# Gated linear attention on one core: the key-value product moved ahead of the query-key product in every turn

## The reference, cut to what matters

```
q, k, v = (x @ Wq.T), (x @ Wk.T), (x @ Wv.T)          # each as (b, s, 16, 64)
log_decay = -softplus(x @ Wd.T + bd)
k_gated = k * sigmoid(x @ Wg.T)
s_t = exp(log_decay_t) * s_{t-1} + k_gated_t^T v_t      # the state, one per head
o_t = q_t s_t
out = o * rsqrt(mean(o*o) + eps) * norm_w
out = out * sigmoid(x @ Wog.T)
return out @ Wo.T
```

## Time and profile before

| | |
|---|---|
| median of three runs | 2803.56 us |
| lowest and highest of them | 2798.45 and 2810.31 us |
| the profiled execution | 2810.31 us, span 2808.5 us |
| PE busy over the span | 86% |
| mean granted clock of PE, as a share of full speed | 0.922 |

### The profile page before, as it was taken

The page is one execution under the profiler, slowest core; times in us unless marked ns, Lnnn a source line. Parts: engine busy times, 40 slices in busy tenths (PEclk is TensorE's granted clock), DMA queues, the critical chain, the costliest instruction groups (busy, mean ns, idle before and its releaser), DMA issues. The chain is left out here.

```text
span 2808.5 us, 35462 instructions
## 1 busy us (share of the span) xinstructions
PE 2412.8 (86%) x14123; PEld 1671.5 (60%) x14131; DVE 1471.8 (52%) x2517; ACT 862.3 (31%) x1247; POOL 505.0 (18%) x420
## 2 busy tenths in 40 slices
PE   5877775778888979988999998839999799999888
PEld 3655663432222767865667666736667577777764
DVE  7996876558774340125564564571110355455543
ACT  1111556424556112324442432201221232222132
POOL 3332330040001113420100001102221210101010
PEclk8989887988999979999999999859999899999999
DMA  3001100054340016633321221032231300000000
GB/s 111 1 0 65 42 16 16 7 125 90 63 63 26 14 62 236 235 114 105 96 64 64 87 73 33 25 114 72 100 101 57 106 18 17 12 12 17 1 33 30
DMA packets 73254, 177.16 MB, mean 63 GB/s; under 512 B 16759, under 2 KB 36728, under 8 KB 67545
## 3 DMA queue, kind: packets, MB, share of 16 engines
q1 hardware_dynamic: 60562, 123.00, 15.4%
q0 software_dynamic: 10368, 50.01, 5.2%
q10 hardware_dynamic: 2176, 2.10, 0.2%
HBM read 149.45 MB, written 25.43 MB: 62 GB/s over the span
## 5 line engine op out<-in xcount | busy, mean ns | idle before, releaser
L1621 PE MATMUL L_ffn_h_ps<-L_ffn_xgT,L_ffn_w 128*128 128x512 f32 (+2 forms) x992 | 232.5, 391 | 6.7 <-DVE L_ffn_xgT L1704 5.7
L1633 PE MATMUL L_ffn_y_ps<-L_ffn_w,L_ffn_h 128*128 128x256 f32 x1008 | 222.5, 380 | 4.8 <-issue 3.9
L526 DVE TENSOR_REDUCE L_attn_neg<-L_attn_Y 128x1 f32<-128x512 f32 (+3 forms) x304 | 187.4, 658 | 59.0 <-PE L_attn_Y L399 57.5
L1633 PEld LDWEIGHTS L_ffn_y_ps<-L_ffn_w,L_ffn_h 128*128 128x128 f32 x1008 | 189.7, 190 | 33.1 <-issue 8.2
L1679 ACT ACTIVATE L_ffn_h<-L_ffn_h_ps,L_ffn_w 128x640 f32<-128x640 f32 (+2 forms) x184 | 101.5, 552 | 347.4 <-PE L_ffn_h_ps L1621 321.7
L1621 PEld LDWEIGHTS L_ffn_h_ps<-L_ffn_xgT,L_ffn_w 128*128 128x128 f32 x992 | 154.4, 193 | 84.2 <-issue 69.3
L496 ACT ACTIVATE L_attn_room<-L_attn_Y 128x1024 f32<-128x1024 f32 (+1 forms) x192 | 147.4, 812 | 82.3 <-PE L_attn_Y L450 81.6
L399 PE MATMUL L_attn_Y<-L_attn_K,L_attn_Q 104*128 104x512 bf16 (+3 forms) x384 | 120.6, 365 | 44.1 <-DVE L_attn_neg L526 24.9
L1713 DVE TENSOR_TENSOR L_ffn_yg<-L_ffn_y_ps,L_ffn_w 128x256 f32<-128x256 f32 x63 | 26.7, 425 | 223.5 <-PE L_ffn_y_ps L1633 223.5
L1704 DVE COPY L_ffn_xgT<-L_ffn_t_ps 128x256 f32<-128x256 f32 x63 | 24.6, 421 | 215.1 <-PE L_ffn_t_ps L1608 199.8
L1754 POOL DMA_INDIRECT token_outputs<-L_ffn_yg,puts x63 | 61.8, 981 | 325.3 <-DVE L_ffn_yg L1713 325.3
(11 more groups left out here) (561 smaller groups left out, 4977.1 us busy)
## 6 DMA issues: line engine op xcount, KB each, us to landing
L_ffn_w<-in_L_ffn_w SPq DMA_DIRECT2D x8, 2180.0 KB
L_attn_bc<-decays SPq DMA_DIRECT2D x32, 512.0 KB, 5.9
L_attn_bp<-decays SPq DMA_DIRECT2D x32, 256.0 KB, 6.8
L_attn_Q<-L_attn_q_parts SPq DMA_DIRECT2D x48, 128.0 KB, 4.7
L_attn_K<-L_attn_k_parts SPq DMA_DIRECT2D x48, 128.0 KB, 6.7
L_attn_first_w<-in_L_attn_w SPq DMA_DIRECT2D x8, 640.0 KB
L_attn_w<-in_L_attn_w SPq DMA_DIRECT2D x8, 640.0 KB, 3.9
token_outputs<-zero SPq DMA_DIRECT2D x1, 4096.0 KB, 20.6
```

The lines of the kernel that those rows point to most:

```text
L526: nc.vector.tensor_reduce(neg[:, c, j0:j0 + heads, tt], R[n % 2][:, 0:heads * width(tt, c)].rearrange("p (h k) -> p h k", h=heads), X_AXIS ...
L1621: ins = nc.tensor.matmul(h_ps[f % 2][:, lo // CW, 0:hi - lo], w1[g % NB][:, kt, f * P:(f + 1) * P], xgT[u][:, kt, lo:hi], start=kt == 0, s ...
L1633: ins = nc.tensor.matmul(y_ps[k % 2][:], h[:, f, t * P:(t + 1) * P], w2[g % NB][:, f, :], start=f == 0, stop=f == FT - 1)
```

## The change

In the table JOBS, `kv` moves from third place to first, and the buffers are dealt anew: `kv` goes to X2 where `s0` was, and `s0` to X3 where `kv` was. The waits that `buffer_read` derives follow: `kv` now waits for the read of `og` from X2, and the pair s0/s1 for the read of `kt` from X3. On DVE the masking of kv moves ahead of the two multiplications of s0 and s1, and the wait for `read["kt"]`, which is DVE's own, goes. No instruction is added, removed or resized.

```
-        JOBS = [("s0", 0, 2), ("s1", 0, 0), ("kv", 0, 3), ("q", 1, 1), ("g", 1, 2), ("k", 1, 3), ("out", 0, 0),
+        JOBS = [("kv", 0, 2), ("s0", 0, 3), ("s1", 0, 0), ("q", 1, 1), ("g", 1, 2), ("k", 1, 3), ("out", 0, 0),
                 ("v", 1, 1), ("og", 1, 2), ("kt", 1, 3)]
...
                 if has_this:
-                    dve.wait_ge(read["kt"], n + 1)
+                    dve.wait_ge(mm["kv"], n + 1)
+                    V.tensor_tensor(kv[:], chunks(X[BUF["kv"]])[:, 0:CH - 1, :], over(same[:], CH - 1), ALU.mult).then_inc(read["kv"], 1)
                     for j in range(2):
                         dve.wait_ge(mm["s1"], n + 1)
                         V.tensor_tensor(bc[par][j][:], chunks(X[BUF[f"s{j}"]]), bc[par][j][:], ALU.mult).then_inc(read[f"s{j}"], 1)
-                    dve.wait_ge(mm["kv"], n + 1)
-                    V.tensor_tensor(kv[:], chunks(X[BUF["kv"]])[:, 0:CH - 1, :], over(same[:], CH - 1), ALU.mult).then_inc(read["kv"], 1)
                     past(dve, mm["out"], n)
```

## The result

| | before | after |
|---|---|---|
| median of five runs, us | 2803.56 | 2819.90 |
| lowest and highest, us | 2798.45, 2810.31 | 2814.05, 2822.70 |
| ratio after / before, 95% interval | | 1.0053 (1.0032 to 1.0075) |
| the profiled execution, us | 2810.31 | 2812.25 |

The changed kernel is slower, by 16.3 us from median to median; the interval of the ratio makes that 9 to 21 us. The forecast was 2820. The profiled execution of the changed kernel is not one of the five. In a second comparison on another occasion it was 2817.84 against 2800.72, ratio 1.0060 (1.0046 to 1.0074). The two profiled executions differ by only 1.9 us, and that would mislead: the part with the change lengthened by 21 us while the rest of the program, which the change doesn't touch, was 19 us shorter in the one than in the other.

A forecast was written before the change was run, and what follows sets the result against it. PE was taken to bound each turn by its instructions plus its waits. Terms 13.9 + 0 + 2.0 + 0.5 = 16.4 us slower, on the median of 2803.56, gave 2820 us; range 2808 to 2834.

The forecast's parts named there:

- The wait of kv: Behind the transposes, kv waits for kd: 1.43 us idle in place of 0.44, in 14 turns, 13.9 us (13.2 to 16.1).
- The neighbours: Durations of s and kv on PE in their new order: taken as unchanged, up to 1.7 us either way over 14 turns.
- Turn 0: First turn, kd late: s no longer hidden in kv's gap, 2.0 us more (1.5 to 3.6).
- Turn 15: Last turn: out waits for states that DVE makes after reading s and kv, 0.5 us more (0.3 to 0.8).
- The sum: All terms over this part of the program: 16.4 us slower.
- the main term: Middle-turn borders where kv waits for kd: 14 x 0.99 = 13.9 us slower.
- Not exposed: PE begins s while kv waits, so s covers kd as now: 2803.6 us, no loss; chance 0.05.
- DVE late: Multiplications and states shift by 1.0 us, v waits 0.3 to 0.5 us in 15 turns: 2826 us; chance 0.12.
- The room left: Slack between DVE's scaled query and the start of v after the change: forecast as 0.2 us.
- The clock falls at each border: Each wait ahead of kv costs clock, 1.63 us in 14 turns: 39 us slower in all, 2843 us; chance 0.07.
- Given back elsewhere: Slow-clock pattern behind the part falls differently; if 8 us come back, the time is 2812 us; chance 0.16.

The follow-up runs named there:

- the one with an instruction more: Changed kernel with one extra DVE instruction, half the size of kd and its result unused, ahead of kd; one run took 2840.72 us.
- the deal alone: Kernel before with s0 dealt to X3 and kv to X2 as in the changed kernel, s still first; one run took 2819.92 us.
- the run with the late mask: Changed kernel with DVE masking kv behind the two multiplications and its own wait for the kt read as before; one run took 2830.30 us.
- before with two instructions more: Kernel before with two extra DVE instructions, each about 0.60 us and unused, ahead of kd; one run took 2802.24 us.

## Why the prediction was right, and where its terms were not

*The wait of kv* was predicted as 1.43 us in place of 0.44, 14 times. It is 1.43, 14 times, in both traces of the changed kernel, and the 0.10 us of way was right too. That the cover of s is the cause is shown: the same delay of `kd` costs nothing where s stands before kv and 0.60 us where kv is bare, and the cover ends where it was put, at about 1.0 us.

*The neighbours* were taken as zero, with 0.12 us either way. They cost 27.24 - 26.09 - 0.99 = 0.16 to 0.17 us a turn, 2.3 over 14, where the bound was 1.7. This is the term that was mis-sized, and the trace had rows for it only in the old order. Why kv takes 0.07 and the projections 0.10 more in the new order is open.

*Turn 0* was put at 2.0 (1.5 to 3.6). From the start of the transposes to `out` it takes 21.3 and 21.7 us in the traces of before, 24.4 and 24.6 after: 3.0. The gap grew to 6.9 and 7.5 us, and kv and s together take 6.0 and 5.8 us in place of 1.73 + 1.99 = 3.72, so the slow stretch costs 2.3 and 2.0 where it cost 1.6 before: in the direction of the upper end. The term itself varies from trace to trace; kv first in the old buffers, with a gap of 6.0, took 23.6.

*Turn 15* was put at 0.5 more, by a chain of 8.96 us from kv to `out`; it is 1734.19 - 1725.31 = 8.88, where before the start of s and that of `out` lay 8.41 apart: 0.47. The wait of `out` is 5.09 and not about 5.3, against 4.59 before, and `out` is slow behind it, as it was before. The timeline of PE after, which answers to the earlier trace rows:

```profile
1734.19 3.33 PE L2336 MATMUL L_attn_X<-L_attn_qd,L_attn_st 128*128 128x128 f32 x14 [5.09 <-DVE L_attn_st L2459]
1737.45 3.33 PE L2341 MATMUL L_attn_X<-L_attn_bc,L_attn_va 128*64 128x128 f32 x32
```

From there to the part's last transposes it is 48.4 and 48.2 us after, 46.7 and 44.1 before: 2.9 more. The longer wait is not the reason that the traces bear out: kv first in the old buffers has the same 5.09 and takes 45.5, and the one with an instruction more has it too and takes 44.4, while the deal alone, with 4.59, takes 45.8. How the slow stretches fall there differs from trace to trace.

*The sum.* 14 x 1.155 = 16.2, then 3.0 and 0.5 make 19.7, where the traces have 19.6 up to the last `out`; the forecast had 16.4 for the same terms, some 3 us too little, of which the neighbours are 2.3 and turn 0 is 1.0. The measured time is 16.3 and in the second comparison 17.1, and both intervals (9 to 21 and 13 to 21 us) hold 16.4 as well as 19.6. So that the median came out within 0.1 us of the forecast is luck; the direction, the place and the main term were right on their own.

*The rivals.* Not exposed: refuted, in every turn. DVE late: it did not happen, and the run with the late mask shows that 1.2 us more would have cost 0.7 to 0.8 a turn. The room left was 0.53 us, or 0.4 less the 0.1 for the way, where 0.2 had been forecast. The clock falls at each border: it did not, the granted clock is 1.00 from 1320 to 1722; but one step further, at 2.03 us, it falls behind 5 waits of 14. The prediction's own evidence was better than it said: the 0.97 of the earlier trace rows comes from its last 4 us (0.70 from 541 to 545, behind a wait of 2.17 us), while from 500 to 541, with the waits of 1.35 us, the clock is 1.00. The section of the Trainium skill weighed there ("TensorE: Matmul & The Clock Gate", "A second HAM failure mode: psum-queue depth-cycling") has the clock swing where small idle times stand between groups of matmuls. The traces agree with it at 2.03 us, and at 3.82, if that is still small; they do not at 1.43 to 1.58, where none of 70 waits in five traces was followed by a lower clock. Given back elsewhere: seen in the first pair of traces, and not separable from chance.

## What to carry to other kernels

On an engine that takes its work in order, the job placed right behind the maker of another engine's input should be one that needs neither that engine's result nor the buffer it is reading; here such a job of 1.99 us covered a way there and back of 1.43. When buffers are dealt by a table, read off for each job which reader it waits for: a wait that comes from the buffer and not from the data can be dealt away. And when a prediction is met, compare the part and not only the whole.

## What had not been expected of the hardware

The start of s at a border comes 0.25 us behind the engine that ends its wait, be it ACT or DVE: it began 0.26 us after ACT's gate and, with the deal alone, 0.25 after DVE's `kd`, where kv needs 0.10 behind the same `kd`. The prediction had laid the 0.26 on ACT. What makes the difference is open; in turn 8 s and kv alike start 0.05 us after the last x_tok listed.

Without any wait the period fell by 0.51 us and not by 0.44. From the start of the transposes to that of s it is 1.48 us with the wait and 0.97 (1387.85 to 1388.82) without, so s starts before the listed end of the transposes (1.04), and the idle time in brackets is short of what the wait costs by that overlap.

A wait of 2.03 us in 27.85 is enough to lower the clock in some turns and not in others, with the same work around it; where it falls, it costs 1.57 us, more than the lengthening of the wait that brought it on. Nor does it take such a wait: in before with two instructions more, the granted clock fell (0.79 from 1494 to 1502) at the output projection of turn 7, behind an idle time of 0.29 us and 16 products of a single column, which take 1.8 us. The projection took 29.56 us there and 27.87 in the same place of before, where the same rows stand ahead of it.
